# The fourth scan of a turn is moved to the head of the next turn on VectorE, in a two-layer kernel with a state-space branch and 64 experts

## The reference, cut to what matters

```python
def step(state, inp):                       # for every token, over T=512 tokens of each of 4 rows
    dt_t, u_t = inp
    A_bar = jnp.exp(dt_t[..., None] * A)    # A = -exp(A_log), 128 x 16
    state = A_bar * state + dt_t[..., None] * B_mat * u_t[..., None]
    y_t = jnp.einsum('bhn,hn->bh', state, C_mat) + D_vec * u_t

def body(acc, p):                           # for each of the 64 experts
    W1, B1, W2, B2, e = p
    h = jax.nn.silu(xf @ W1 + B1) @ W2 + B2
    cw = jnp.sum(jnp.where(ti == e, tw, 0.0), axis=-1)
    return (acc + cw[:, None] * h, None)
```

## Time and profile before

| | us |
|---|---|
| median of 3 runs | 524.03 (523.99 to 524.27) |
| the profiled execution, its own time | 524.22 |
| its span, first to last instruction | 522.4 |
| stretch of the 8 turns, first table load to last weighing | 364.2 to 507.9 |
| busy share of the span: TensorE, VectorE, ScalarE, GpSimd | 85%, 73%, 53%, 37% |

### The profile page before, as it was taken

One profiled execution on the slowest core, in us unless ns is written; L12 is line 12 of the kernel. 1 busy time (PEld: TensorE's weight loads), 2 busy tenths in 40 slices (PEclk: granted clock), 3 DMA queues, 4 the chain that ended last, 5 costly groups with the idle time before them and its releaser, 6 DMA issues.

```text
span 522.4 us, 7319 instructions
## 1 busy us (share of the span) xinstructions
PE 442.2 (85%) x2143; PEld 325.9 (62%) x2143; DVE 382.8 (73%) x702; ACT 278.1 (53%) x392; POOL 194.8 (37%) x188
## 2 busy tenths in 40 slices
PE   2729999999999999999989969299689778977893
PEld 1327887888878888788877845155455445544452
DVE  5687478944888448894498987776768877887784
ACT  2375674426644275533655255835676577557730
POOL 1248014400144001530002100740477778777850
PEclk9958999999999999999999979579799999999997
DMA  6420001100012000000000000000265776687664
GB/s 177 96 61 23 2 0 43 43 1 0 0 41 52 0 0 0 0 0 0 1 0 2 1 0 1 0 2 0 55 130 114 144 141 131 116 157 137 126 130 120
DMA packets 29535, 26.76 MB, mean 51 GB/s; under 512 B 10837, under 2 KB 25414, under 8 KB 29510
## 3 DMA queue, kind: packets, MB, share of 16 engines
q0 software_dynamic: 4608, 16.78, 16.8%
q1 hardware_dynamic: 24902, 9.69, 7.3%
HBM read 8.64 MB, written 1.05 MB: 19 GB/s over the span
## 4 chain that ended last, share of the span: by engine, by line
PE 29%; DVE 28%; POOL 19%; issue 13%; ACT 7%; DMA 2%; DVEq 1%; SPq 0%; POOLq 0%; ACTq 0%
POOL state L435 9%; PE psum L1083 7%; PE psum L203 6%; PE psum L205 6%; PE psum L204 6%; POOL xn_tok L439 4%; POOL g_hi L448 3%; DVE hid L771 2%; PE psum L1203 2%; DVE at_m L800 1%; DVE at_m L802 1%; POOL g_lo L449 1%; DVE xn_tok L693 1%; POOL sel_now L450 1%; PE psum L1218 1%
## 5 line engine op out<-in xcount | busy, mean ns | idle before, releaser
L567 ACT ACTIVATE sil<-psum 128x512 f32<-128x512 f32 (+1 forms) x96 | 56.3, 596 | 104.3 <-PE psum L205 91.2
L771 DVE TENSOR_TENSOR hid<-sil,psum 128x512 f32<-128x512 f32 (+1 forms) x96 | 65.1, 686 | 51.8 <-PE psum L205 32.9
L1083 PEld LDWEIGHTS psum<-e_w,hid 128*128 128x128 f32 (+1 forms) x768 | 94.9, 191 | 6.0
L1083 PE MATMUL psum<-e_w,hid 128*128 128x128 f32 (+1 forms) x768 | 95.3, 274 | 0.0
L203 PE MATMUL psum<-xn_hi,e_hi 128*128 128x512 f32 (+1 forms) x192 | 81.8, 426 | 7.9 <-DVE hid L771 7.3
L975 DVE TENSOR_TENSOR_SCAN state<-dec,win_t 128x1024 f32<-128x1024 f32 x32 | 73.4, 2295 | 20.0 <-ACT dec L643 20.0
L205 PE MATMUL psum<-xn_lo,e_hi 128*128 128x512 f32 (+1 forms) x192 | 76.0, 396 | 0.0
L204 PE MATMUL psum<-xn_hi,e_lo 128*128 128x512 f32 (+1 forms) x192 | 75.8, 395 | 0.0
L652 ACT ACTIVATE sil<-psum,vec_t 128x512 f32<-128x512 f32 x64 | 43.2, 687 | 47.3 <-PE psum L205 36.8
L435 POOL TENSOR_SCALAR state<-state,ssm_cb 128x1024 f32<-128x1024 f32 x32 | 49.7, 1552 | 45.2 <-DVE state L975 42.2
L1258 PE MATMUL psum<-hid,g_w 128*128 128x512 f32 x128 | 61.3, 592 | 0.0
(11 more groups left out here) (261 smaller groups left out, 766.5 us busy)
## 6 DMA issues: line engine op xcount, KB each, us to landing
xn_tok<-state POOLq DMA_DIRECT2D x32, 512.0 KB, 4.5
e_raw<-in_L_ffn_w SPq DMA_DIRECT2D x16, 128.0 KB, 2.1
e_raw<-in_L_ffn_w SPq DMA_DIRECT2D x8, 176.0 KB, 2.4
res<-in_L_attn_x SPq DMA_DIRECT2D x4, 256.0 KB, 3.9
g_raw<-in_L_ffn_w SPq DMA_DIRECT2D x16, 64.0 KB, 2.3
g_w<-in_L_ffn_w SPq DMA_DIRECT2D x16, 64.0 KB, 2.5
out<-res SPq DMA_DIRECT2D x4, 256.0 KB, 2.9
e_raw<-in_L_ffn_w SPq DMA_DIRECT2D x16, 48.0 KB, 1.9
```

Source lines behind the costliest of these rows:

```text
L567: act.activation(sil[0:M, s % 2, :], ps[s % 2][0:M, :], ACT.Silu).then_inc(silu_done, 1)
L771: dve.tensor_tensor(hid[0:M, tb % 2, ft, :], sil[0:M, s % 2, :], ps[2 + s % 2][0:M, :], ALU.mult).then_inc(gated, 1)
L1083: ins = pe.matmul(ps[4 + o % 2][:, n * P:(n + 1) * P], hid[0:m, tb % 2, ft, n * P:(n + 1) * P], e_w2[j][0:m, ft, :], start=(ft == 0), stop ...
```

## The change

Scans and weighings keep their operands, waits and number. Only VectorE's order changes. The fourth scan of a turn, `scan(i, 3)`, moves behind the last weighing of its turn and so directly ahead of `scan(i+1, 0)`; the weighings between the remaining scans become three, three and two.

```diff
             for i in range(NG // GPI):
                 c = i * GSTEPS
-                for k in range(SCANS):
-                    scan(i, k)
-                    for s in range(2 * k, 2 * k + 2):
-                        weigh(c + s)
+                if i > 0:
+                    scan(i - 1, 3)
+                scan(i, 0)
+                for s in (0, 1, 2):
+                    weigh(c + s)
+                scan(i, 1)
+                for s in (3, 4, 5):
+                    weigh(c + s)
+                scan(i, 2)
+                for s in (6, 7):
+                    weigh(c + s)
+            scan(NG // GPI - 1, 3)
```

## The result

| | before | after |
|---|---|---|
| median us (lowest to highest of 4 runs each) | 524.15 (523.99 to 525.00) | 530.48 (529.92 to 532.02) |
| profiled execution: own time, span | 524.22, 522.4 | 530.41, 528.6 |

The ratio after to before is 1.0122, with a 95% interval of 1.0098 to 1.0146. The change makes the kernel 6.3 us slower. It was forecast as slower, at 534.2. The range of 523.5 to 538.5 held the result, but the number is 3.7 too high.

What follows compares the result with a forecast made beforehand. A turn was the SiLU chain plus 6.51, with scans and GpSimd compute excluding each other. One free turn (-0.67), trapped turns (+6.0) and tail (+4.9) gave +10.2 on 524.22: 534.4, stated as 534.2 us; range 523.5 to 538.5.

Steps and rivals of the forecast that it cites:

- the gain: SiLU chain: weighing 2 no longer behind scan 1, SiLU 5 at +6.0, turn 17.03, 0.67 less if nothing else moves.
- the trap: GpSimd's cast misses scan 1 by some 0.15 and ends behind it, delaying TensorE's unit 4: turn 19.03, 1.33 more.
- the push: Scan 2's multiply, caught by scan 3, delays next turn's scan 0 to R' - 0.05; without it scan 0 ends 0.8 earlier.
- 4.5 x 1.33 = + 6.0: Cost of trapped turns: the remaining four to five turns, each 1.33 longer, add 6.0 us.
- Every other turn: Rival: longer trapped turns let GpSimd catch up, so the next is free, three of each; 529 to 531, chance 0.17.
- the tail: After the last turn's SiLUs: scan 3, multiply and DMA issue end 4.9 later, or 2.9 if the turn went undisturbed.
- TensorE's clock falls: Rival: idling some 2.6 before unit 4 lowers TensorE's clock, 0.9 a turn, 4.5 over five; 539, chance 0.10 with shut-out.
- most turns trapped: Main forecast: the cast misses scan 1 in three to six turns; 531 to 537, chance 0.52.
- GpSimd shut out across both scans: Rival: no multiply slips between scans 3 and 0, cast ends near +6.3; +16, 540, chance 0.10 with clock.
- The cast gets through: Rival: the cast passes scan 1 in every turn; -1.1, so 522.9, chance 0.15.

Runs made afterwards that it cites:

- preparation-first kernel: Changed kernel with the second group's preparation moved ahead of the fourth scan's multiply on GpSimd: 528.41 us, 1.0087 against the kernel before.
- the weighing alone: Kernel before with weighing 2 ahead of scan 1 but scan 3 kept ahead of weighings 6 and 7: 521.54 us, 0.9947.

## Why the prediction was right, and where its number was off

**Right, the gain.** 17.03 for a free turn; turns 2 and 4 have 17.06 and 17.07. In turn 2 it comes by the step named, SiLU 5 at +6.03 behind weighing 3. In turn 4 it is partly luck: the later cast (+2.91) holds unit 4, SiLU 4 starts at +4.31 and SiLU 5 at +6.10 behind its own product, and this path happens to be as long. The kernel without multiplies has SiLU 4 at +3.62 to +3.65 and SiLU 5 at +6.02 or +6.03 in every turn, as predicted.

**Right, the trap and its price.** Predicted for a trapped turn: cast to +5.44, SiLU 4 at +6.45, turn 19.03. Measured in turn 3: +5.44, +6.54, 19.12. The two ends of the push are there too. The prediction put the cast at +3.03 with the push and 0.8 earlier without; measured +3.23 behind a pair of 5.33, and +2.19 behind a pair of 4.54.

**Wrong, how many turns are trapped.** The term "4.5 x 1.33 = + 6.0" rests on "I expect it to be caught again", the multiply of scan 2 beside scan 3 in every turn, with the full push of 0.8. The push is not the same in each turn. Ahead of turn 1 it is nothing, ahead of turn 2 it is 0.45 (4.99 less 4.54), ahead of turn 3 it is 0.79. A turn with the full gain is 17.06 long, and GpSimd falls further behind from one turn to the next, until a cast misses the scan. The trapped turn lasts 19.12 or 20.71, and GpSimd catches up in it, a little in the first (next cast at +2.91), fully in the second, which the clock made longer (next cast at +2.19). Two turns of six were trapped, not 4.5. What ran is close to the rival *Every other turn*, which I gave 0.17. Its 529 to 531 holds the result, though its "three of each" is not what the turns show: two trapped, two with the full gain, two with none.

**A term that I left out.** Turns 1 and 6 had time for the cast and no gain. The 1.12 multiply of scan 0 then stands just ahead of scan 1, which takes 2.88. I had costed GpSimd's effect on scan 0, never on scan 1. The preparation-first kernel shows this meeting in every turn.

**Too high, the tail.** 4.9 forecast, 3.2 measured. The last turn was free, for which the text had 2.9.

**Too low, the clock.** Of the rival *TensorE's clock falls* one turn in two came true. It cost 1.6 in turn 5, more than the 0.9 taken from turn 0's excess over the others.

**Put together.** The turns 1 to 6 cost + 3.05 (two trapped, one with the fall of the clock, two free, two without gain), where I had + 5.3; the tail cost 3.2, where I had 4.9. The start and turn 0 cancel (- 0.35, + 0.35). That is the 3.9 between the forecast 10.2 and the measured 6.3, but for 0.1. The forecast's own range for most turns trapped, 531 to 537, lies just above the result, and that it is so near is in part luck: without the fall of the clock (1.6), which the sum did not have, the time would have been about 528.9.

**Refuted.** *GpSimd shut out across both scans*: the multiply slipped in between, the pair took 5.33, and the trapped turn was 19.12 and not 20. *The cast gets through* is what four of the six turns did (1, 2, 4 and 6), two of them with the full gain, and what the kernel without multiplies does everywhere. In one detail I was too strict: the text had the cast miss unless it had 0.19 before it touches the gate, and a start 0.16 ahead of scan 1 was enough.

**The shared interfaces.** The section Specifications of the Trainium skill's page "GPSIMD Engine Reference" says that GpSimd's SBUF interfaces are shared with VectorE, with contention for VectorE instructions that have two SBUF inputs. The runs agree: the turns 1 to 6 last 17.05 to 17.07 without the multiplies and 17.06 to 20.71 with them. They show more than a sharing, since each held instruction waits for the other's end.

## What to carry to other kernels

- An idle gap on one engine can be the slack of another that shares a resource with it. Before filling it, list who holds the resource in that stretch. Here VectorE's idle 2.16 was the time in which GpSimd caught up.
- When a reorder has two parts, run each alone: separate the half that brings the late instruction forward from the half that fills the gap. Here the first alone gave 0.9947, the second alone 1.0110 (times as a share of the kernel before).
- A short instruction that gates another engine (a cast of 0.29) must not be within a few tenths of a long one at the same gate. Move the long one away or the short one well ahead; both together gave 0.9925. Moving the short one ahead by itself gave only 1.0087, as it pushed other work onto the scan.
- Work that moves to a later place in every turn also moves the end of the loop. Here this tail was 3.16 of the 6.2, and 2.91 even without the multiplies.

## What the runs showed of the hardware

- A scan of 128x1024 and a compute instruction of GpSimd hold each other off until the other has ended, in both directions and for tiny ones as well: a 128x128 cast of 0.29 took 2.21, a multiply of 1.12 took 3.12, and a scan of 2.28 behind a multiply took up to 3.58. A waiting multiply gets in between two back-to-back scans (5.33 instead of 4.54).
- Tenths of a microsecond decide who goes first: a cast that started 0.16 behind a scan was held, one 0.16 ahead was not. But the start in the row is not the moment that decides. With the weighing alone, a multiply that starts 0.01 behind scan 0 (420.36, 420.35) went first. In the order before without multiplies, GpSimd's `g_hi` was held by a scan that starts 0.21 later:

```profile
394.35 2.58 POOL L446 TENSOR_SCALAR g_hi<-g_raw 128x128 fp32r<-128x128 f32 x1
```

```profile
394.56 2.28 DVE L973 TENSOR_TENSOR_SCAN state<-dec,win_t 128x1024 f32<-128x1024 f32 x1
```

- As GpSimd falls behind in free turns and catches up in trapped ones, a kernel whose list repeats has turns of 17.06 and 20.71 side by side. One turn read from the trace does not stand for the others.
- TensorE's granted clock fell to 0.50, the 1.2 GHz level, behind a wait of 2.64 and behind waits of 1.96, but not behind waits of 2.65 and 1.59. What decides is open.
